# Moving the Gelu and the attention copy in ScalarE's order, and a slot's scores ahead of its transposed probabilities on TensorE

## What is computed

```python
for i in range(6):
    x = attn_layer(shift_tokens(x), Wqkv[i], q_scale[i], k_scale[i], Wo[i]) + x
    x = ffn_layer(shift_tokens(x), ln_g[i], ln_b[i], W1[i], b1[i], W2[i], b2[i]) + x

# attn_layer: 16 heads of 64; q, k = l2norm(...) * scale, then rotary
sim  = einsum('bhwie,bhwje->bhwij', bq, bk2) * 8.0      # windows of 32, own and the one before
attn = softmax(where(mask, -big, sim), -1)
out  = einsum('bhwij,bhwje->bhwie', attn, bv2) @ Wo
# ffn_layer: layer norm, then a * gelu(gate, approximate=False) @ W2 + b2
```

## Time and profile before

| | |
|---|---|
| median of 3 runs | 1858.72 us (1857.57 to 1862.71) |
| the profiled execution's own time | 1855.56 us |
| its span, first to last instruction | 1853.8 us |
| busy: PE, PEld, DVE, ACT, POOL | 90%, 70%, 77%, 73%, 70% |
| mean granted TensorE clock | 0.978 |
| fill, ahead of the first `less_max` | 93.7 us |

### The profile page before, as it was taken

How to read it: one execution, slowest core, us unless ns; L and a number is a source line. 1 busy time by engine, 2 the same in 40 slices (tenths; PEclk the granted TensorE clock), 3 DMA queues, 4 the chain that set the end, 5 groups by cost and what they waited for, 6 DMA issues and landing times.

```text
span 1853.8 us, 68588 instructions
## 1 busy us (share of the span) xinstructions
PE 1663.1 (90%) x25968; PEld 1291.5 (70%) x26160; DVE 1430.3 (77%) x3041; ACT 1344.7 (73%) x2656; POOL 1293.3 (70%) x1283
## 2 busy tenths in 40 slices
PE   7889999999999999999999999999999999999973
PEld 5667777777777777677777777767777776777751
DVE  4588878878778787887778778788777777778755
ACT  4267777777777777777777777777777777777753
POOL 5287777777777777777777777777777777677720
PEclk9799999999999999999999999999999999999995
DMA  5011111111101011110111101111110111101000
GB/s 164 11 38 34 32 33 32 30 40 48 32 28 34 28 41 46 33 30 28 34 45 41 34 28 30 31 47 37 33 34 29 33 37 32 30 24 30 25 14 20
DMA packets 41406, 66.13 MB, mean 36 GB/s; under 512 B 7072, under 2 KB 16032, under 8 KB 41376
## 3 DMA queue, kind: packets, MB, share of 16 engines
q1 hardware_dynamic: 40224, 65.38, 11.7%
q10 hardware_dynamic: 1152, 0.34, 0.1%
HBM read 20.61 MB, written 1.05 MB: 12 GB/s over the span
## 4 chain that ended last, share of the span: by engine, by line
PE 68%; ACT 11%; issue 10%; DVE 9%; POOL 1%; ACTq 1%; DMA 0%; DVEq 0%
PE ps_a L490 11%; PE ps_f L490 11%; PE ps_qs L490 9%; PE ps_po L490 8%; PE ps_q L490 7%; PE ps_k L490 5%; PE ps_v L490 5%; PE ps_po L604 4%; PE ps_qs L596 3%; PE ps_tk L596 3%; ACT L906 2%; DVE ssq L1084 2%; DVE prob L1121 2%; ACT p_bd L838 2%; ACT squares L844 2%
## 5 line engine op out<-in xcount | busy, mean ns | idle before, releaser
L426 POOL TENSOR_TENSOR qk<-qk,rnorm 128x512 f32<-128x512 f32 x384 | 393.1, 1045 | 298.2 <-DVE rnorm L1111 298.2
L418 POOL TENSOR_TENSOR qk<-qk,qk_rot 128x512 f32<-128x512 f32 x384 | 483.7, 1276 | 111.1 <-DVE qk_rot L1078 110.8
L1084 DVE TENSOR_REDUCE ssq<-squares 128x8 f32<-128x512 f32 x384 | 257.6, 680 | 71.1 <-ACT squares L844 58.2
L490 PE MATMUL ps_qs<-k_t,q_t 64*32 64x64 f32 x12288 | 210.7, 218 | 67.6 <-ACT k_t L838 46.5
L838 ACT COPY p_bd<-ps_po 64x512 f32<-64x512 f32 x384 | 221.3, 576 | 34.7 <-PE ps_po L604 32.4
L433 POOL TENSOR_TENSOR prob<-prob,row_inv 128x512 f32<-128x512 f32 x192 | 200.3, 1043 | 51.5 <-DVE row_inv L1130 51.5
L1127 DVE TENSOR_REDUCE row_sum<-prob 128x8 f32<-128x512 f32 x192 | 131.7, 686 | 120.6 <-ACT prob L944 120.6
L490 PEld LDWEIGHTS ps_qs<-k_t,q_t 64*32 64x32 f32 x12288 | 179.7, 107 | 57.2 <-issue 57.2
L944 ACT ACTIVATE prob<-prob 128x512 f32<-128x512 f32 x192 | 121.2, 631 | 110.9 <-DVE prob L1121 107.6
L490 PEld LDWEIGHTS ps_po<-p_bd,v_back 128*64 128x64 f32 x3072 | 162.9, 137 | 49.5 <-issue 31.8
L490 PE MATMUL ps_po<-p_bd,v_back 128*64 128x64 f32 x3072 | 193.9, 225 | 1.6 <-ACT p_bd L838 1.5
(11 more groups left out here) (161 smaller groups left out, 4002.6 us busy)
## 6 DMA issues: line engine op xcount, KB each, us to landing
v_back<-v_own SPq DMA_DIRECT2D x192, 192.0 KB, 2.4
w_raw<-in_wqkv SPq DMA_DIRECT2D x48, 192.0 KB, 2.4
v_back<-v_own SPq DMA_DIRECT2D x96, 64.0 KB, 2.1
wo_sb<-in_wo SPq DMA_DIRECT2D x12, 256.0 KB, 3.0
w_sb<-in_w SPq DMA_DIRECT2D x6, 341.0 KB, 3.4
w_sb<-in_w SPq DMA_DIRECT2D x6, 192.0 KB, 2.7
x_in<-in_x SPq DMA_DIRECT2D x4, 256.0 KB, 5.0
out<-s_out SPq DMA_DIRECT2D x8, 128.0 KB, 1.9
```

The costliest lines, as they stand in the source:

```text
L418: nc.gpsimd.tensor_tensor(qk[:, s, i, :], qk[:, s, i, :], qk_rot[:, s, i, :], ALU.add).then_inc(added, 1)
L426: nc.gpsimd.tensor_tensor(heads(qk[:, s, i, :]), heads(qk[:, s, i, :]), rnorm[:, s, 8 * i:8 * i + 8].unsqueeze(2).to_broadcast([P, 8, HEAD ...
L490: return nc.tensor.matmul(o, lhs, rhs, start=start, stop=stop, **kw)
L1084: V.tensor_reduce(ssq[:, s, 8 * i:8 * i + 8], heads(squares[:, s, OCTET * i:OCTET * i + OCTET]), AX, ALU.add).then_inc(ssq_done, 1)
```

## The change

ScalarE: `keep_turned` is split. The copy of queries (`keep_queries`) stands first in the slot; behind it now stands `keep_attention`, which had been the last but one in the slot before; then the copy of keys (`keep_keys`). The Gelu of a batch moves from the end of slot 0 to slot 1, behind the copy of keys, and there alone `keep_p` comes right behind Gelu and ahead of the squares. In slot 0 `keep_p` no longer stands between the squares of q and of k but behind both. TensorE: `scores` of unit `u - 2` comes ahead of `turn_p` of unit `u - 3`. Nothing is computed otherwise than before, and no instruction is added.

```diff
@@ TensorE, in body(n) @@
                     if j == 2 and live_batch(n - 3):
                         ff_down(n - 3)
+                    if live(u - 2):
+                        scores(u - 2, (j - 2) % UNITS, j % 2)
                     if live(u - 3):
                         turn_p(u - 3, (j - 3) % 2)
-
-                    if live(u - 2):
-                        scores(u - 2, (j - 2) % UNITS, j % 2)
                     if j == 1 and live_batch(n - 1):
                         out_projection(n - 1, 0)
@@ ScalarE @@
-            def keep_turned(u, j, s):
-
-                octet, tile = j // 2, j % 2
+            def keep_queries(u, s):
+
                 wait(act, s_done, u - 1)
                 act.wait_ge(tq_done, u + 1)
                 copy(q_t[:, s, :], ps_qs[:]).then_inc(q_turned, 1)
+
+            def keep_keys(u, j):
+
+                octet, tile = j // 2, j % 2
                 act.wait_ge(tk_done, u + 1)
                 copy(k_t[:, octet, :, WINDOW + P * tile:WINDOW + P * tile + P],
                      ps_tk[:].rearrange("p (c t) -> p c t", t=P)).then_inc(k_turned, 1)
@@ ScalarE, in body(n) @@
                     if live(u - 2):
-                        keep_turned(u - 2, (j - 2) % UNITS, j % 2)
+                        keep_queries(u - 2, j % 2)
+                    if live(u - 4):
+                        keep_attention(u - 4, n - 1, j)
+                    if live(u - 2):
+                        keep_keys(u - 2, (j - 2) % UNITS)
+                    if j == 1 and live_batch(n - 3):
+                        gelu(n - 3)
+                        if live(u - 3):
+                            keep_p(u - 3, (j - 3) % 2)
                     if live(u):
                         squares_of(u, 0, j % 2)
-                    if j == 0 and live(u - 3):
-                        keep_p(u - 3, (j - 3) % 2)
-                    if live(u):
                         squares_of(u, 1, j % 2)
-                    if j > 0 and live(u - 3):
+                    if live(u - 3) and not (j == 1 and live_batch(n - 3)):
                         keep_p(u - 3, (j - 3) % 2)
@@
                     if live(u):
                         keep_v(u, n, j)
-                    if live(u - 3):
-                        keep_attention(u - 3, n if j >= 3 else n - 1, (j - 3) % UNITS)
-                    if j == 0 and live_batch(n - 3):
-                        gelu(n - 3)
```

## The result

The changed kernel takes 1933.24 us (median of 4 runs, 1931.05 to 1936.41) against 1859.95 (4 runs) before: 1.0395 times the time, 95% interval 1.0373 to 1.0416. The forecast was 1926 with a range of 1885 to 1955, and slower. The profiled execution has a span of 1931.1 us, 77.3 more than before.

What follows compares the result with a forecast made beforehand. The prediction took the `less_max` chain, with ScalarE full in slot 1, as the bound: slot terms of 1.54, taken as 1.48 us a step, over 45 steps give 67, with the ends 68, so about 1926 us, range 1885 to 1955.

Steps and rivals of the forecast that it cites:

- That TensorE's idle in slot 1 would come back as a wait for `less_max`: Slot 1: TensorE's 1.57 us of idle goes, but returns as a wait before q is turned in slot 2.
- The rival by which TensorE is the bound: Slot 1: the 1.57 us of TensorE idle vanishes and nothing replaces it, 1788 us, faster; chance 0.08.
- Slot 1 gets 0.63 us longer: Slot 1, ScalarE's reordered chain: the norms' root comes at 934.00, not 933.37; 0.63 us longer, bounds 0.3 and 0.9.
- Slot 2 gets 1.12 us longer, because Ln waits behind p_bd: Slot 2: p_bd is copied later, Ln waits behind it, `less_max` starts 1.12 us late; bounds 0.8 and 1.3.
- the small piece that I had named beside it: Slot 2, TensorE: `values` wait a little for p_bd, so slot 3 starts 0.21 us late.
- its -0.21: Slot 3: `less_max` is 0.91 us late after 1.12 in slot 2, so 0.21 shorter; bounds -0.5 and +0.1.
- The swap as the larger part: Slots 2 and 3, scores ahead of turned probabilities: terms of 1.12 and -0.21 in a sum of 1.54 us a step.
- Slot 0 worth nothing: Slot 0: squares of k come 0.5 us earlier but the root comes as before; 0, bounds -0.1 and +0.1.
- The sum: Whole step: 0.63 + 1.12 - 0.21 + 0 = 1.54 us longer, taken as 1.48; bounds 0.5 and 2.4.
- The drain: End of the run: one table load is saved, 1.3 us shorter.
- The attention copy costs nothing: ScalarE, every slot: moving the attention copy costs nothing, 0.5 us of work before and after, its readers come later.

Runs made afterwards that it cites:

- Gelu late: Kernel before with Gelu at the end of slot 1, Ln and Exp's table loaded again in slot 2, GpSimd's gate moved to slot 2: 1888.09 us.

## Why the prediction was right, and where it was not

**That TensorE's idle in slot 1 would come back as a wait for `less_max`.** Right, and seen at its place: 1.32 us before q is turned in slot 2, for some 1.6 forecast. The 1.57 us that the prediction took for the idle before holds a mask's matmul of 0.30 which that trace doesn't have; the idle was about 1.27. For the same reason TensorE's share is 89% and not the 87% forecast. The rival by which TensorE is the bound needed the root in slot 1 to come 1.6 us earlier; it came 0.9 later.

**Slot 1 gets 0.63 us longer.** The sign and the chain were right, the size was 0.93, just over the term's own bound of 0.9. The missing 0.30 is no part of slot 1's own walk. Nearly all of it is slot 0's edit, which makes slot 1 0.28 longer with the swap and without it, and which I had booked at 0: I looked only at when the root comes there, which indeed did not change (8.14 against 8.21 us), and not at `values`, which wait 0.89 us for p_bd. TensorE then begins slot 1 late and turns q 0.39 us after the end of `less_max`, not 0.06. With TensorE's old order that edit costs 0.19 us a step. With the swap it saves 0.71, since it spares the squares of k the wait behind a late p_bd. Of slot 1's 0.94 (medians), ScalarE's order without slot 0's edit makes 0.48, slot 0's edit 0.28 and the swap 0.18.

The reason given for slot 1, that ScalarE's sum of work holds it, is borne out by p_bd's place behind the squares, where only 0.33 us of waits and lost overlap was gained. It is half of the matter. Leaving out the tables showed a second chain of nearly the same length through VectorE's sums of squares, which I hadn't seen.

**Slot 2 gets 1.12 us longer, because Ln waits behind p_bd.** The length is right (1.20 measured) and its meaning was wrong. What fails is that this delay of `less_max` enters the sum as a cost. With Ln ahead of p_bd slot 2 is 1.24 us shorter and slot 3 as much longer, and the time is the same. What carries the delay out of slot 2 is TensorE alone, in the small piece that I had named beside it: `values` wait for p_bd. The sum of the two slots was right all the same (0.91 forecast, 0.92 measured), and not by luck: slot 3 was walked from TensorE's start, 0.21 late, and its -0.21 is the 0.91 at its end less the 1.12, so the 1.12 cancels. By that walk 0.21 of the 0.91 comes out of slot 2, and 0.70 is made in slot 3 by its own swap. Added slot by slot the attribution misleads, the sum does not.

**The swap as the larger part.** Undoing it takes 1.09 of 1.79 us. By the terms it was 0.91 of 1.54 and some of slot 1, so the proportion held.

**Slot 0 worth nothing.** For its own length, yes (-0.07); for the step, no, as told.

**The sum.** 1.54, which I rounded down to 1.48 because terms for overlap "lean upwards"; measured 1.78. That lowering had no row behind it. The drain was forecast 1.3 us shorter and is 5.2. It is as short with the swap undone (61.4 us behind the last `less_max`, 66.6 before) and 63.2 with the attention copy alone, so it comes with ScalarE's order; these are single profiles. The two errors partly cancel: 45 times 0.30 is 13.5 us too little, the drain 3.9 too much. Like for like, the profiled executions lie 77 us apart, for 68 forecast. The medians lie 73 apart, because the profiled execution before was 4.4 us under its median and the one after 0.3. That 1926 came within 7 us of 1933 owes something to luck: 9 us too little in the sum, and 3 too much for the way from the profiled execution to the median.

**The attention copy costs nothing.** Right in the steps, 35.71 us against 35.69; the whole is 0.9985 of before.

## What to carry to other kernels

Price an order by what reaches the next stage on the engine that is full there, not by how late each event in between comes: a delayed event that something later absorbs is no cost, however long its row says that somebody waited. When two orders on two engines are changed together, walk each alone as well: here the swap alone costs 8.9%, on top of the order that goes with it 2.8% (1.0395 over 1.0116). Before moving work out of a wait, ask which chain is second: in slot 1 one of two nearly equal chains could be taken away for next to nothing, while Gelu at the end of slot 1, with slot 2 reordered on four engines by reading each new wait, gave 1.3%. And compare a kernel's steps with each other before taking a median or one step for all: in the swap alone two kinds alternate.

## What the runs showed of the hardware

TensorE's granted clock fell to 1.2 GHz in the swap alone, in nearly every second step, behind waits of 0.83 and 1.88 us in slot 1. In the neighbouring step, with waits of 0.84 and 1.89 at the same places, it was 1.00. Where it fell the transpositions took 1.06 us in place of 0.66 and the step 0.71 more. In the change, with waits of 1.32 and 0.45, and with Gelu late, with waits of 1.30 and 0.37, it was 1.00 in all full steps.

A table load takes 1.28 us on ScalarE, starts 0.01 to 0.02 after the instruction before it has ended and holds the next for 0.01 to 0.02 more. Whether it costs anything hung on the order alone: two loads a step were worth 1.15 us in the kernel before and 0.17 in the changed one.
